# Normalising roots by bits and Newton steps on GpSimd, a four-bit feed-forward in pairs with silu on ScalarE, and a rotary attention unrolled

## The reference, cut to what matters

```python
# four-bit feed-forward (twice); blocks of 16 values share a scale
scale = max(max(abs(xb)) / 6.0, 1e-12)
xq = GRID[searchsorted(MID, abs(xb / scale))] * sign(xb) * scale
h = silu(xq @ gate_q) * (xq @ up_q)      # 352 wide
y = quantised(h) @ down_q

# forgetting attention: 16 heads of 64, q and k normalised head by head
q = q / sqrt(mean(square(q)) + 1e-6) * qnw      # k alike, after a convolution of 4 taps
p = softmax(q k' / 8 + cum_t - cum_s, causal)
out = p @ v
out = out / sqrt(mean(square(out)) + 1e-6) * onw * (g * sigmoid(g))

# rotary attention: 16 heads of 8, q and k rotated and scaled to length 1
out = softmax(q k' * 8 ** -0.5) @ v
```

## Time and profile before

| | us |
|---|---|
| median of 3 runs (lowest, highest) | 2471.85 (2471.19, 2473.13) |
| the profiled execution: its own time; its span | 2476.36; 2474.6 |
| busy PE / DVE / ACT / POOL in the span | 1943.5 / 1648.7 / 1395.7 / 1013.6 |
| first feed-forward, fx and fh stages, from the span's start | 429.6 to 476.1, 476.1 to 621.5 |
| second, the same | 729 to 776, 776 to 921.6 |
| forgetting attention, its loop over units | 962 to 2006.4 |
| rotary attention, `rt_` | 2158.6 to 2439.4 |

### The profile page before, as it was taken

One profiled execution on the slowest core, in us unless ns is written; L12 is line 12 of the kernel. 1 busy time (PEld: TensorE's weight loads), 2 busy tenths in 40 slices (PEclk: granted clock), 3 DMA queues, 4 the chain that ended last, 5 costly groups with the idle time before them and its releaser, 6 DMA issues. The chain is left out here.

```text
span 2474.6 us, 37339 instructions
## 1 busy us (share of the span) xinstructions
PE 1943.5 (79%) x11731; PEld 880.3 (36%) x11731; DVE 1648.7 (67%) x2449; ACT 1395.7 (56%) x2254; POOL 1013.6 (41%) x818
## 2 busy tenths in 40 slices
...
DMA packets 66132, 85.94 MB, mean 35 GB/s; under 512 B 13345, under 2 KB 37217, under 8 KB 65889
## 3 DMA queue, kind: packets, MB, share of 16 engines
...
## 5 line engine op out<-in xcount | busy, mean ns | idle before, releaser
L1975 ACT ACTIVATE rt_p<-rt_ps_s 128x1024 f32<-128x1024 f32 x256 | 242.7, 1026 | 43.8 <-PE rt_ps_s L1912 43.1
L1618 DVE SCALAR_TENSOR_TENSOR fu_kv<-fu_ps_kv,fa_vec,fu_kv 128x511 f32<-128x511 f32 x366 | 252.6, 739 | 7.3 <-ACT fu_kv L1526 6.4
L1690 POOL TENSOR_TENSOR fu_p<-fu_p 128x768 f32<-128x768 f32 x64 | 116.9, 1826 | 260.3 <-PE fu_ps_n L1376 256.0
L1346 PE MATMUL fu_ps_s<-fu_qn,fu_kn 64*128 64x512 f32 (+3 forms) x1024 | 190.0, 468 | 7.3 <-ACT fu_p L1513 5.6
L601 POOL TENSOR_TENSOR scan_hC<-scan_h,scan_c 128x1024 f32<-128x1024 f32 x64 | 150.8, 2356 | 82.7 <-DVE scan_h L581 82.7
L1376 PE MATMUL fu_ps_n<-fu_p,fu_vt 128*64 128x512 f32 (+3 forms) x1024 | 166.0, 445 | 0.0
L526 PE MATMUL scan_ps_y<-scan_hC,w_ident 128*128 128x512 f32 x256 | 130.3, 632 | 40.9 <-POOL scan_hC L601 24.3
L1701 POOL TENSOR_TENSOR fu_num<-fu_num,fu_sg 128x512 f32<-128x512 f32 x64 | 81.4, 1272 | 172.1 <-DVE fu_sg L1651 172.1
L581 DVE TENSOR_TENSOR_SCAN scan_h<-scan_dA,scan_ps_b 128x1024 f32<-128x1024 f32 x64 | 146.4, 2287 | 2.2
L1923 PE MATMUL rt_ps_o<-rt_p,rt_va 128*32 128x512 f32 x1024 | 138.1, 612 | 4.6 <-POOL rt_va L1900 3.5
L1404 PE MATMUL fu_ps_kv<-w_XN,fa_wp 128*128 128x512 f32 x244 | 125.1, 636 | 18.1 <-DVE fu_cr L1583 15.4
...
## 6 DMA issues: line engine op xcount, KB each, us to landing
fu_rb<-rms_rows SPq DMA_DIRECT2D x256, 128.0 KB, 2.9
fu_ro<-rms_rows SPq DMA_DIRECT2D x128, 128.0 KB, 2.9
...
```

The costliest lines, as they stand in the source:

```text
L1346: pe.matmul(sps[:, h, at:at + T - t * P], k[head(h), t * P:(t + 1) * P], q[head(h), t * P:T], start=(at == 0), stop=False)
L1618: dve.scalar_tensor_tensor(acc, projected(a, k)[:, 0:T - j], vec[:, a % GA, at:at + 1], acc, ALU.mult, ALU.add).then_inc(done, 1)
L1690: pool.tensor_tensor(tail, tail, P13[:, :, 0:3 * P], ALU.add).then_inc(s.d1, 1)
L1975: act.activation(pr[k % 2][i][:, :, :], sps[i][:, :, :], ACT.Exp, scale=DH_B ** -0.5).then_inc(s.exp, 1)
```

## The change

Three stages are rewritten.

1. Forgetting attention. The variances are folded: 32 x 512 rows become 128 wide (`VAR`, 96x128) by 4 transfers on SP. VectorE makes a first guess of the root by a shift and an exclusive or of the bits (L1658), and POOL does two Newton steps in 11 dependent instructions (L1726 to L1747), between the sums `ds` (L1720) and the gated product `fu_num` (L1751). The Ln, the Exp and the table loads are gone. QN is moved behind the maxima, and two lists that were ordered otherwise in the window iteration have their common order.
2. Feed-forward. Silu comes from ScalarE; tiles go in pairs; `mag` is on VectorE, 128x704 at a time (in fx 128x1024); gates and ups are issued two tiles ahead; there are 4 `up` buffers instead of 3, one `tps` instead of two, and the lag of the turn is 4 tiles instead of 3.
3. Rotary attention. All loops are unrolled, scores have three PSUM buffers, the value products follow two steps behind and stand between the two score pairs, the output has one PSUM buffer instead of two.

```diff
@@ fh: scalar
-                            act.activation(th[j % NT][:, :, :].rearrange(flat), gps[j % 2][:, :], ACT.Tanh, scale=0.5).then_inc(s.th, 1)
+                        act.activation(gt[j % NT][:, :, :].rearrange(flat), gps[j % 2][:, :], ACT.Silu).then_inc(s.gt, 1)
@@ fh: vector
-                        dve.scalar_tensor_tensor(gt[j % 2][:, :, :].rearrange(flat), th[j % NT][:, :, :].rearrange(flat), 1.0, gps[j % 2][:, :], ALU.add, ALU.mult).then_inc(s.gt, 1)
-                        dve.scalar_tensor_tensor(tot[j % 2][:, :, :], size[j % 2][:, :, :], ROUND, ups[j % 3][:, :, :], ALU.max, ALU.add).then_inc(s.tot, 1)
+                        dve.tensor_scalar(mag[k % 2][:, :, :, :], size[k % 2][:, :, :, :], ROUND, None, ALU.max).then_inc(s.mag, 1)
+                        dve.tensor_tensor(tot[j // 2 % 2][:, j % 2, :, :], mag[j // 2 % 2][:, j % 2, :, :], ups[j % 4][:, :, :], ALU.add).then_inc(s.tot, 1)
@@ fh: gpsimd
-                        pool.tensor_scalar(mag[j % 2][:, :, :], size[j % 2][:, :, :], ROUND, None, ALU.max).then_inc(s.mag, 1)
@@ forget_units: sync, before the put
+                                sp.dma_start(VAR[32 * g:32 * g + 32, :], MS[32 * g:32 * g + ROWS, :]).then_inc(s.fold, 16)
@@ forget_units: scalar
-                        act.preload_act_table_set("natural_log_exp_and_others")
-                        act.activation(MS[r, :], MS[r, :], ACT.Ln).then_inc(s.ln, 1)
-                        act.activation(R[j % 2][r, :], MS[r, :], ACT.Exp, scale=-0.5).then_inc(s.r, 1)
@@ forget_units: vector, behind the last taps
+                        dve.tensor_scalar(ROOT[r, :].bitcast(I32), VAR[r, :].bitcast(I32), 1, 0x7fffffff, ALU.logical_shift_right, ALU.bitwise_xor).then_inc(s.bits, 1)
@@ forget_units: gpsimd, ahead of the gated product (a wait ahead of each)
+                        pool.tensor_scalar(y, y, ROOT_SCALE, None, ALU.mult).then_inc(s.ya, 1)
+                        pool.tensor_tensor(e, y, y, ALU.mult).then_inc(s.yb, 1)
+                        pool.tensor_tensor(e, e, x, ALU.mult).then_inc(s.yc, 1)
+                        pool.tensor_scalar(e, e, -0.5, 1.5, ALU.mult, ALU.add).then_inc(s.yd, 1)
+                        pool.tensor_tensor(y, y, e, ALU.mult).then_inc(s.y1, 1)
...
+                        pool.tensor_tensor(R[j % 2][r, :], y, f, ALU.mult).then_inc(s.r, 1)
@@ rope_attend
+        RING = 3
+        sps = [st.ps(f"s{k}", [P, 2, T]) for k in range(RING)]
+        ops = st.ps("o", [P, T])
@@ rope_attend: tensor
-                            scores(n, k, 1)
-                            if k:
-                                values(n, k - 1)
+                        if n is not None and k >= 2:
+                            values(n, k - 2)
...
+                        if n is not None:
+                            scores(n, k, 1)
```

More of the change, by code:

```diff
@@ L836, in end @@
                         i.then_inc(s.t, 1)
-                        if t == NT - 1:
-                            pe.wait_ge(s.ht, 2 * (j + 1))
-                            pe.wait_ge(s.x, m)
-                            for c in range(KF):
-                                rows = min(P, FF - c * P)
-                                i = pe.matmul(yps[:, :], w.down[0:rows, c, :], HT[m % 2][0:rows, c, :], start=(c == 0), stop=(c == KF - 1))
-                            i.then_inc(s.y, 1)
-                    gate(0)
@@ L846, in _, with down @@
-                    for j in range(G + LAG):
-                        if real(j + 1):
-                            gate(j + 1)
-                        if real(j):
-                            up(j)
-                        if real(j - LAG):
-                            end(j - LAG)
+                    def down(m):
+                        pe.wait_ge(s.ht, 2 * NT * (m + 1))
+                        pe.wait_ge(s.x, m)
+                        for c in range(KF):
+                            rows = min(P, FF - c * P)
+                            i = pe.matmul(yps[:, :], w.down[0:rows, c, :], HT[m % 2][0:rows, c, :], start=(c == 0), stop=(c == KF - 1))
+                        i.then_inc(s.y, 1)
@@ L854, in _ @@
+                    gate(0)
+                    gate(1)
+                    up(0)
+                    up(1)
+                    for j in range(G + LAG + 1):
+                        if real(j + 2):
+                            gate(j + 2)
+                            up(j + 2)
+                        k = j - LAG
+                        if real(k):
+                            turn(k)
+                        if k >= NT and k % NT == 0:
+                            down(k // NT - 1)
                 @block.scalar
@@ L867, in _ @@
+                            act.wait_ge(s.mag, max(j // 2 - 1, 0))
+                            act.activation(size[j // 2 % 2][:, j % 2, :, :], ups[j % 4][:, :, :], ACT.Abs, scale=STEP).then_inc(s.size, 1)
                         k = j - LAG
@@ L902, in _, with maxima @@
[L902 to L907 removed]
+                        dve.tensor_tensor(h, gt[j % NT][:, :, :].rearrange(flat), h, ALU.mult).then_inc(s.h, 1)
+                    def maxima(j):
+                        dve.wait_ge(s.h, j + 1)
+                        dve.tensor_reduce(amax[j // 2 % 4][:, j % 2, :], ups[j % 4][:, :, :], AX_X, ALU.max, apply_absolute_value=True).then_inc(s.amax, 1)
@@ new lines, in _ @@
+                    for k in range(G // 2 + 1):
+                        both = (2 * k, 2 * k + 1) if k < G // 2 else ()
+                        for j in both:
+                            product(j)
+                        if k:
+                            sizes(k - 1)
+                            total(2 * k - 2)
+                            total(2 * k - 1)
+                        for j in both:
+                            maxima(j)
+                        if both:
+                            scales(k)
+                        for j in both:
@@ L1272, in forget_units @@
         MS = st.sb("ms", [96, T])
-        R = [st.sb(f"r{k}", [96, T]) for k in range(2)]
+        VAR, ROOT, STEP1, STEP2 = (st.sb(n, [96, CUT]) for n in ("var", "root", "step1", "step2"))
+        R = [st.sb(f"r{k}", [96, CUT]) for k in range(2)]
         kvps, sps, mps = (st.ps(n, [P, 2, T]) for n in ("kv", "s", "m"))
         nps, ssps = st.ps("n", [P, T]), st.ps("ss", [P, T])
-        s = st.sems("set ones kvp tap t1 t2 cv th sk sv vt vc qp qc q2 k2 sa so dsq msq mso ln r rb ro put cr0 cr1 cr2 qn kn qm km "
+        s = st.sems("set ones kvp tap t1 t2 cv th sk sv vt vc qp qc q2 k2 sa so dsq msq mso fold bits ya yb yc yd y1 ye yf yg yh yi r rb ro put cr0 cr1 cr2 qn kn qm km "
                     "mx red hi ml rt rr sc ex pv d1 d2 ds n2 nc gp tg sg gated og wo x")
@@ L1895, in _ @@
                 pool.wait_ge(s.ones, 1)
-                with pool.Fori(0, B) as i:
-                    wait_apart(pool, w, s.pv, STEPS * i)
+                for i in range(B):
+                    pool.wait_ge(s.pv, STEPS * i)
                     for t in range(NT):
@@ L1995, in step @@
                     if last is not None:
+                        take(last, GROUPS - 1)
                         norm(last, GROUPS - 1)
```

264 lines of the change are left out of this document (143 added, 121 removed).

## The result

The changed kernel takes 2525.7 us (median of 4 runs, 2525.08 to 2532.69) against 2471.5 of before: a ratio of 1.0227, 95% interval 1.0207 to 1.0248. It is slower by 54 us. The forecast was slower by 19, 2491 with a range of 2437 to 2530: the sign and the range hold, the size is less than half of what came.

A forecast was written before the change was run, and what follows sets the result against it. PE sets the pace in the forgetting attention, no engine is full in the feed-forward, PE and ACT alternate in the rotary attention; 79 - 42 - 1 - 17 = +19 on 2471.85 gives 2491 us, range 2437 to 2530.

The forecast's parts named there:

- the added part: Forgetting attention: work added and the root's new time; QN delays the last taps by 0.7, R ends 6.7 us later.
- The late root: Forgetting attention: OG waits for RO, PE stalls 4.0 us, a window costs 4.3 net; stage +79 us.
- The feed-forward: Main feed-forward stage: DVE's pair takes 6.1 instead of 7.2, stage 124 instead of 145.4; -42 us for both runs.
- The quantising stage: fx of the feed-forward: `mag` goes from POOL to DVE; -1 us for both runs, -8 to +4.
- The rotary attention: Rotary attention: third score buffer lets PE run ahead and shrinks ACT's waits; 264 instead of 281, -17 us.
- the short chain: Rival, forgetting attention: POOL's 128-wide operations cost what its copy does, chain 4.2, stage +40; 2452 us, chance 0.15.
- ACT as the bound: Rival, forgetting attention: table switches bound the windows and the late root is caught, -32 - 60; 2380 us, chance 0.03.
- the port: Rival, feed-forward: `mag` and one-input operations on DVE lock out POOL, feed-forward gains only 10; 2523 us, chance 0.11.
- the low clock: Rival, forgetting attention: the clock stays low longer after each stall, +2 a window; 2520 us, chance 0.08.

The follow-up runs named there:

- qn_alone: The kernel before with only QN moved behind the first maxima, roots still by Ln and Exp: 2518.6 us (1.0187 of before).
- qn_split: The changed kernel with QN back in its old place in all iterations but the one behind a window: 2481.7 us (1.0035 of before).
- one_step: The changed kernel with the second Newton step left out, 5 chain instructions instead of 11: 2455.2 us (0.994 of before).
- ro_ahead: The changed kernel with outputs normalised one iteration later and RO's load ahead of the folding transfers and the put on SP: 2486.5 us (1.0055 of before).
- ring_alone: The kernel before with the changed feed-forward and rotary attention, but value products one step behind, after both score pairs: rotary attention 267.1 us.

## Why the prediction was right and where it failed

**The step that failed** is one sentence of the added part: "QN then stands ahead of the last taps, which end 0.7 later". QN's price there was taken from the place it left, 0.73, and its move was followed in the window iteration alone. It is moved in all 64. In the window iteration the price was nearly right (0.89). In the ordinary ones it meets POOL's 128x768 sum near its beginning and takes 2.28, and these iterations, which the sum held at nothing, cost 37.8 us (28 of them, +15.8 and +22.0); qn_alone measures 45 for the move alone, qn_split 39 of the stage for its undoing there. The warning stood in the rows used: L1602 of 1.85 beside POOL, against 0.73.

**The late root was right** in its mechanism and, in part by luck, in its size. Bits 11.4 behind RR (forecast 11.5), chain 5.54 (6.2; the two forms with two immediates 0.29 instead of 0.53), OG 5.4 behind R (5.3: the put landed in 1.5 instead of 2.1, what followed took that much longer), PE's wait 2.73 in the iteration shown and 3.5 on the mean (4.0: it came for the maximum ahead, and I had it wait for L1627), the clock behind it 0.57 (as the earlier trace rows), window iteration 16.48 (16.47), pair of iterations 35.1 (35.3). All of the stage that is not the ordinary iterations is 77.4 where the sum had 79. That is closer than its terms: the chain and the wait came out shorter, and what PE loses besides waiting larger, some 1.5 us an iteration instead of 1.1 less 0.3; and QN's place behind the window is in the 77.4. one_step and ro_ahead show the late root as the cause, each by another end of the chain.

**The feed-forward was undersized**, 57.5 instead of 42: a pair that doesn't wait lasts 5.2 and not 6.1, since I gave up the overlap of neighbouring instructions. That is 14 us in each of the two; the waits for `up` behind the first tile, 13.6 instead of 10, take a part of it back. PE's clock rose to 0.89 in it (0.82); what that gave is not shown. The price of `mag`, 0.53, came out at 0.519.

**The quantising stage had the wrong sign**, +6.3 instead of -1: again an instruction of DVE (`above`, 0.2) set beside one of POOL. I had seen that L896 waits for POOL and counted it where POOL's work leaves, not where it comes.

**The rotary attention** gave 13.2 of 17: right in kind. That the order of the values has no part in it ring_alone shows; that it is the buffer and not the unrolling is read from the traces.

**Of the rivals** the short chain fell (5.54, not 4.2); ACT as the bound fell with the wait that OG did get; the port came true, but in fx and in QN rather than in the feed-forward's `q`, and the feed-forward gained 57.5 and not 10. That the port's 2523 and the low clock's 2520 lie next to 2525.7 is luck. The errors of the terms were +36 (the ordinary iterations 38, the root -2), +7, -16 and +4, together +32 of the 35 us between forecast and result.
